# Unread products at the borders of a four-part transformer kernel, with joined loads at its start and another order at the start of its last attention

## The reference

```
x = LN(x + attn0(x))   # 16 heads of 8: softmax(q k^T / sqrt(8) - distance, causal) v, then Wo
x = LN(x + moe(x))     # argmax over 8 experts; LN, 128 -> 512 relu -> 128 of the chosen expert
x = LN(x + attn1(x))   # 16 heads of 64: RMS-normed q, k; bias -distance * omega * softplus(gate(k)); causal
x = LN(x + ffn(x))     # silu gate, two 512x512 gelu layers, 512 -> 128
```

## Time and profile before

| | us |
|---|---|
| median of 3 runs (lowest, highest) | 2205.83 (2204.8, 2212.89) |
| the profiled execution's own time | 2213.37 |
| its span | 2211.6 |
| TensorE busy | 2041.5 (92%) |
| VectorE, ScalarE, GpSimd busy | 1389.9, 1146.0, 839.6 |
| mean granted clock of TensorE | 0.952 |

### The profile page before, as it was taken

One profiled execution on the slowest core, in us unless ns is written; L12 is line 12 of the kernel. 1 busy time (PEld: TensorE's weight loads), 2 busy tenths in 40 slices (PEclk: granted clock), 3 DMA queues, 4 the chain that ended last, 5 costly groups with the idle time before them and its releaser, 6 DMA issues.

```text
span 2211.6 us, 37667 instructions
## 1 busy us (share of the span) xinstructions
PE 2041.5 (92%) x13392; PEld 1231.1 (56%) x13392; DVE 1389.9 (63%) x3316; ACT 1146.0 (52%) x1859; POOL 839.6 (38%) x544
## 2 busy tenths in 40 slices
PE   5799999998487988896999999999999999999998
PEld 3355455554476544454566666666666665656644
DVE  4788888883632787874677777777777764333311
ACT  2366666666344676782455555555555552232232
POOL 5000000001501445442577777777777772000000
PEclk8799999999589999995899999999999999999999
DMA  5233333113165689897477677767776697433300
GB/s 177 104 128 133 134 130 119 59 54 98 65 188 151 187 268 338 270 287 181 105 180 180 154 177 180 182 161 173 178 182 166 168 223 211 110 86 86 91 5 10
DMA packets 260313, 336.09 MB, mean 152 GB/s; under 512 B 22732, under 2 KB 181756, under 8 KB 259720
## 3 DMA queue, kind: packets, MB, share of 16 engines
q1 hardware_dynamic: 244824, 305.82, 51.6%
q0 software_dynamic: 7664, 24.39, 3.1%
q10 hardware_dynamic: 7640, 3.48, 0.6%
HBM read 193.69 MB, written 122.62 MB: 143 GB/s over the span
## 4 chain that ended last, share of the span: by engine, by line
PE 49%; DMA 2%; SPq 2%; DVE 0%; ACT 0%; issue 0%; DVEq 0%
PE ps L959 11%; PE ps L1296 10%; PE ps L910 7%; PE ps L941 6%; PE ps L942 6%; PE ps L1247 2%; PE ps L947 1%; PE ps L1307 1%; PE ps L922 1%; PE ps L1284 1%; PE ps L1285 1%; SPq L1171 1%; DMA a1QA<-a1QB 1%; DMA a1FQ<-s_q 1%; DMA s_y<-a1raw 0%; DMA fyb<-s_y 0%
## 5 line engine op out<-in xcount | busy, mean ns | idle before, releaser
L1132 POOL TENSOR_TENSOR a1sum<-a1sum,a1prob 128x1024 f32<-128x1024 f32 (+3 forms) x256 | 461.3, 1802 | 101.7 <-ACT a1prob L1075 69.7
L1075 ACT ACTIVATE a1prob<-ps 128x512 f32<-128x512 f32 (+2 forms) x640 | 322.7, 555 | 239.1 <-PE ps L947 206.3
L480 DVE TENSOR_REDUCE a0grid<-ps 128x8 f32<-128x1024 f32 x288 | 346.6, 1222 | 99.4 <-PE ps L350 48.8
L581 ACT ACTIVATE a0prob<-ps 128x1024 f32<-128x1024 f32 x288 | 291.3, 1027 | 159.0 <-PE ps L376 89.2
L1011 DVE CUSTOM_DVE_ANT_0 ps<-ps,c_mask_ij 128x128 f32<-128x128 f32 x496 | 264.6, 551 | 92.0 <-issue 87.7
L959 PE MATMUL ps<-a1prob,a1V 128*64 128x512 f32 (+3 forms) x1536 | 275.5, 501 | 4.9 <-ACT a1prob L1075 4.9
L941 PE MATMUL ps<-a1QA,a1KA 69*128 69x512 f32 (+3 forms) x768 | 272.3, 362 | 4.0 <-DMA a1QA<-a1neg 4.0
L942 PE MATMUL ps<-a1QB,a1KB 128*128 128x512 f32 (+3 forms) x768 | 264.9, 353 | 0.0
L910 PE MATMUL ps<-a1KA,a1QA 68*128 68x128 f32 x744 | 229.4, 385 | 5.0 <-DMA a1KA<-s_g 4.3
L959 PEld LDWEIGHTS ps<-a1prob,a1V 128*64 128x64 f32 x1536 | 103.3, 139 | 174.4 <-issue 140.2
L1014 DVE TENSOR_REDUCE a1mx<-ps 128x1 f32<-128x320 f32 x248 | 146.0, 589 | 60.0 <-PE ps L910 57.2
(11 more groups left out here) (269 smaller groups left out, 3191.7 us busy)
## 6 DMA issues: line engine op xcount, KB each, us to landing
a1FQ<-s_q SPq DMA_DIRECT2D x128, 256.0 KB, 7.8
a1KB<-s_k SPq DMA_DIRECT2D x128, 256.0 KB, 8.6
s_xs<-c_zero POOLq DMA_DIRECT2D x19, 1024.0 KB, 8.9
s_q<-mqkT SPq DMA_DIRECT2D x32, 512.0 KB, 4.0
s_v<-mv SPq DMA_DIRECT2D x32, 512.0 KB, 5.8
s_k<-a1KH SPq DMA_DIRECT2D x32, 512.0 KB, 4.9
s_k<-a1KL SPq DMA_DIRECT2D x32, 512.0 KB, 5.9
a1KA<-s_k SPq DMA_DIRECT2D x64, 256.0 KB
```

The costliest lines, as they stand in the source:

```text
L480: dve.tensor_reduce(grid[g % 2][:, :, a:b + 1:b - a], banks(("max", k)), axis=AX.X, op=ALU.max).then_inc(s1_free, 1)
L581: act.activation(prob[:, :, a:b + 1:b - a, :], banks(("exp", q)), ACT.Exp).then_inc(p_full, 1)
L1075: act.activation(weights_of(g, u)[:, group[0]:group[-1] + 1, off:BANK], both(e, u, group), ACT.Exp).then_inc(weighed, 1)
L1132: pool.tensor_tensor(t[:, :, off:BANK], t[:, :, off:BANK], weights_of(g, u)[:, :, off:BANK], ALU.add).then_inc(summed, 1)
```

## The change

1. A new function, `pass_time`, is one fp32 product of the identity with a broadcast of itself into a bank that nobody reads. It stands on TensorE at these places: once per chunk of the routing ahead of `rank`, with the wait on `picked` now ahead of it; eight times after the totals; thirteen times behind the experts, ahead of the wait for their outputs; at n == LAST one of half size after each of the 24 maximum products and one of full size after the turn.
2. The scratch of `attention0` holds three rows of parts per head, so that a head's operand is one block of 24 rows: q as high, high, low and k as high, low, high. A chunk is stored with six DMAs, and a buffer is loaded with two of 48 rows or four of 24.
3. BK of group 0 is loaded on SP's queue behind Q, and `load_second(1)` goes from chunk 5 to behind the row of group 0.
4. At the end of the projections VectorE does six maxima before the gates instead of twelve; TensorE has eight, a gate transpose, one, a gate transpose, and the rest.
5. In group 0 of `attend_and_finish` the maxima begin in unit 4, the turn and the row are one unit later, ACT's two splits stand behind units 4 and 6, VectorE's low part at unit 8, and SP issues the slopes first and v behind q.

```
+def pass_time(nc, const, bank, tiles):
+    ident = const["ident"]
+    nc.tensor.matmul(bank[:, 0:tiles * P], ident[:, :], ident[:, :].unsqueeze(1).to_broadcast([P, tiles, P]), start=True, stop=True)
...
-            for h in range(H):
-                part(engine, buf, name, g, h, done)
+            b, k = divmod(g, per)
+            for m in range(PAIR):
+                row, to, n = 3 * dim * (k * H + m * PAIR), base_of(m) + FIRST, 3 * dim * PAIR
+                engine.dma_start(buf[to:to + n, :].bitcast(F32), scr[name][row:row + n, b * seq:(b + 1) * seq]).then_inc(done, 16)
...
-                for r, part in enumerate((high, low)):
+                for s, part in enumerate(((high, high, low), (high, low, high))[n]):
...
             batch_stored(sp, 0)
+            sp.wait_ge(cleared_first, 1)
             still(sp, Q[0], "q0", 0, loaded1[0])
+            moving(sp, BK[0], "k0", 0, loaded1[0])
...
-                if c == 5:
-                    sp.wait_ge(cleared, 3)
-                    load_second(sp, 1)
...
-                if 0 < g and g + 1 < GROUPS:
-                    sp.wait_ge(s2_full, NU * g)
+                if g + 1 < GROUPS:
+                    if g > 0:
+                        sp.wait_ge(s2_full, NU * g)
+                    else:
+                        sp.wait_ge(cleared, 3)
                     load_second(sp, g + 1)
...
-            act.wait_ge(cleared_first, 1)
-            batch_stored(act, 0)
-            moving(act, BK[0], "k0", 0, loaded1[0])
...
-    share0 = ([0, 0, 2, 3, 3, 4, 4, 4, 4, 0, 0, 0], [0, 0, 0, 0, 0, 0, 0, 0, 0, 3, 3, 3])
+    share0 = ([0, 0, 0, 0, 4, 5, 5, 5, 5, 0, 0, 0], [0, 0, 0, 0, 0, 0, 0, 0, 0, 0, 4, 5])
...
             for h in range(2):
                 copy_high(1, h)
                 load_a(1, h)
-            load_e(1)
             for k in range(PARTS):
                 load_f(2, k)
+            load_v(1)
...
-                    if u == TILES and g + 2 < G:
+                    if u == (TILES if g > 0 else TURN) and g + 2 < G:
                         lower(g + 2, 0)
...
-                    if g + 2 < G and u in (0, 3):
-                        split(g + 2, (0, 3).index(u))
+                    behind = (0, 3) if g > 0 else (4, 6)
+                    if g + 2 < G and u in behind:
+                        split(g + 2, behind.index(u))
...
+                if 0 < i - 3:
+                    pe.wait_ge(picked, i - 3)
                 if 0 <= i - 3:
+                    pass_time(nc, const, ps[:, 5, :], TILES)
                     rank(i - 3)
...
+            for _ in range(8):
+                pass_time(nc, const, ps[:, 6, :], TILES)
...
+            for _ in range(13):
+                pass_time(nc, const, ps[:, 7, :], TILES)
             pe.wait_ge(ye_full, NT)
...
+                    if n == LAST and kind == "max":
+                        pass_time(nc, const, ps[:, 0, :], 2)
+                    if n == LAST and kind == "turn":
+                        pass_time(nc, const, ps[:, 0, :], TILES)
...
-                    first_maxima(range(NM // 2))
+                    first_maxima(range(AHEAD))
```

More of the change, by code:

```diff
@@ L151, in batch_stored @@
             for c in range(b * seq // CHUNK, (b + 1) * seq // CHUNK):
-                engine.wait_ge(stored[c % PARTS3], 16 * 4 * (c // PARTS3 + 1))
+                engine.wait_ge(stored[c % PARTS3], N_STORE * (c // PARTS3 + 1))
         def load_first(engine, g):
@@ L168, in still, with moving @@
         def still(engine, buf, name, g, done):
-            for h in range(H):
-                part(engine, buf, name, g, h, done)
-        def moving(engine, buf, name, g, done):
-            for h in range(H):
[L176 to L185, removed]
+            b, k = divmod(g, per)
+            for m in range(PAIR):
+                row, to, n = 3 * dim * (k * H + m * PAIR), base_of(m) + FIRST, 3 * dim * PAIR
+                engine.dma_start(buf[to:to + n, :].bitcast(F32), scr[name][row:row + n, b * seq:(b + 1) * seq]).then_inc(done, 16)
+        def moving(engine, buf, name, g, done):
+            b, k = divmod(g, per)
+            for h in range(H):
+                row, to, n = 3 * dim * (k * H + h), base_of(h // PAIR) + FIRST + 3 * (h % PAIR) * dim, 3 * dim
+                engine.dma_start(buf[to:to + n, h % PAIR, :].bitcast(F32), scr[name][row:row + n, b * seq:(b + 1) * seq]).then_inc(done, 16)
         def load_x(part):
@@ L195, in store @@
                 nc.sync.wait_ge(low_full, 2 * c + n + 1)
-                for r, part in enumerate((high, low)):
-                    nc.sync.dma_start(scr[name][r, :, c * CHUNK:(c + 1) * CHUNK], part[c % PARTS3][:, n, :].bitcast(F32)).then_inc(stored[c % PARTS3], 16)
+                rows_of = scr[name].rearrange("(h s d) n -> h s d n", s=3, d=dim)
+                for s, part in enumerate(((high, high, low), (high, low, high))[n]):
+                    nc.sync.dma_start(rows_of[:, s, :, c * CHUNK:(c + 1) * CHUNK], part[c % PARTS3][:, n, :].bitcast(F32)).then_inc(stored[c % PARTS3], 16)
         def sync_program():
@@ L576, in exponentials @@
                     for r in range(PARTS3):
-                        act.wait_ge(stored[r], 16 * 4 * len(range(r, chunks, PARTS3)))
+                        act.wait_ge(stored[r], N_STORE * len(range(r, chunks, PARTS3)))
                 if g > 0:
@@ L810, in load_e, with load_v @@
             nc.sync.dma_start(KA[b][EXT:EXT + 4, :, :].bitcast(F32), slopes).then_inc(loaded_e[b], 16)
+        def load_v(x):
+            b, (n, m) = x % NB, divmod(x, PAIRS)
+            if x >= NB:
+                nc.sync.wait_ge(valued, unit(x - NB, NU - 1) + 1)
             nc.sync.dma_start(V[b][:, :, :], scr["v1"][n * S:n * S + S, m * P:m * P + P].rearrange("(t p) n -> p t n", p=P)).then_inc(loaded_v[b], 16)
@@ L848, in sync_program @@
         def sync_program():
+            load_e(1)
             for h in range(2):
@@ L1105, in scalar_program @@
                         keep_den(g - 1)
-                    if u == (TURN if g > 0 else TURN + 2) and g + 1 < G:
+                    if u == (TURN if g > 0 else TURN + 3) and g + 1 < G:
                         row(g + 1)
@@ L1990, in middle @@
         assert turn_gates[LAST]
+        AHEAD = 6
         line = []
@@ L2000, in middle @@
                 here.append((("xT", "gate")[n % 12 // 11], n // 12 + 1, 0))
-            here += [("max", k, 0) for k in range(NM // 2)] if n == LAST else []
-            here += [("aug", c, 0) for c in turn_gates.get(n, ())]
-            here += [("max", k, 0) for k in range(NM // 2, NM)] + [("turn", 0, 0)] if n == LAST else []
+            here += [("max", k, 0) for k in range(AHEAD + 2)] if n == LAST else []
+            for k, c in enumerate(turn_gates.get(n, ())):
+                here += [("aug", c, 0)] + ([("max", AHEAD + 2 + k, 0)] if n == LAST else [])
+            here += [("max", k, 0) for k in range(AHEAD + 2 + len(turn_gates[n]), NM)] + [("turn", 0, 0)] if n == LAST else []
             after_item[n] = here
@@ L2195, in tensor_last @@
                     multiply(n)
-                for _ in after_item[n]:
+                for kind, a, _ in after_item[n]:
                     job(k)
                     k += 1
+                    if n == LAST and kind == "max":
+                        pass_time(nc, const, ps[:, 0, :], 2)
+                    if n == LAST and kind == "turn":
+                        pass_time(nc, const, ps[:, 0, :], TILES)
         def pair(n):
@@ L2364, in vector_last @@
                         gates_b(event_of[EVENTS[n - late][0]])
-            first_maxima(range(NM // 2, NM))
+            first_maxima(range(AHEAD, NM))
             first_row()
```

12 lines of the change are left out of this document (7 added, 5 removed).

## The result

The changed kernel takes 2184.39 us in the median of four runs (2182.59 to 2186.1), the kernel before 2209.36 (four runs, 2204.8 to 2215.85) beside it: a ratio of 0.9885, 95% interval 0.9854 to 0.9915, 25 us less. On another chip, in a later comparison, it was 0.9884 (0.9864 to 0.9903). It is faster, and by a quarter less than the 34 us forecast; the time lies 2 us above the forecast's own range (2162 to 2182) and inside the wide one (2155 to 2196).

The account below looks back on a forecast made before the run. TensorE, busy 92% of the span, was taken as the bound, with stretches at half clock. Terms 10 + 0 + 1 + 3 + 2 + 18 = 34 us gave 2179 against the profiled execution, 2172 as median; range 2155 to 2196.

Parts of the forecast that it names:

- Start: First attention's start: earlier BK loads 4 us, shorter row wait 4, full clock behind it 3, extra stores -1: gain 10.
- Routing: Products ahead of the ranks: hidden in the ranks' wait at full clock; taken 0, bounds 5 us slower to 3 faster.
- Totals: Eight unread products after the totals fit in 11.05 us of standing: gain 1 us, bounds 3 either way.
- border: Behind the experts: thirteen unread products covered by 13.89 us of standing, first projections at full clock: gain 3 us.
- End of the projections: Maximum products before the last attention: unread products covered at full clock, gates' transposes wait less: gain 2 us.
- Group 0: Last attention's first group: two waits gone 9.2 us, clock 15, less 6 for the late `a1FQ` load: gain 18.
- Rival A: Barrier before group 0: passes don't hold the clock; gain 22 us, time 2184; chance 0.20 together with D.
- B: First attention's start gives nothing, extra stored bytes eating the saved issues; gain 24 us, time 2182; chance 0.13.
- C: Half clock where the passes stand, so they cost time: 10 us slower, 2216; chance 0.07.
- D: The split's load eats group 0's gain, leaving 6 to 8 us; time 2183; chance 0.20 together with A.
- A clock once lost stays lost: Dense TensorE stretches, start and group 0: half clock persists despite full activity; rival A therefore costs 12 us, not 4.
- The signs: Trace checks: clock slices, first L350 and L382 times, wq products at 1.9, group 0 at 35 to 39 us, split waiting.

Follow-up runs that it names:

- the two orders alone: Kernel before with only the new orders at the end of the projections and in group 0, no unread products, old start: ratio 0.9956.
- the start alone: Kernel before with only three-part scratch, joined loads, BK on SP's queue and load_second(1) behind the first row: ratios 0.9953 and 0.9947.

## Why the prediction was right or wrong

The time, 2184.39 us, lies in the range and on the forecast side; by the ratio it is 25 us where 34 were forecast. The sum came as near as it did partly by luck: the start gave more than its term in the trace, and group 0 and the routing gave less. Point by point:

- *Start, 10 forecast.* 15 in the trace, 10 to 12 timed alone. The mechanism held, the shares didn't: I gave 4 to the move of `load_second`, which is worth at most about 1 once the loads are joined. Six issues took 2.4 us and not 3.4. Of the price of the larger loads the good end came: TensorE starts 3.8 us behind the last issue of BK, not 9.9.
- *Routing, 0 forecast.* A loss of 1 to 2, within the bounds. The failed step is "a pass at full clock is hidden in the ranks' wait". It stands behind the wait on `picked`, so the wait doesn't cover it; and the clock fell to half there with the passes too.
- *Totals 1, border 3 forecast.* 0.5 and 0.8. The eight were covered as worked out. At the border the clock was down when wq came, 3.76 us as before, behind a stand of 2.65 us that was left after the thirteen. So the step "I expect all to" run at full held for the thirteen (11.3 us), and what it was to buy, the first projections at 1.88, didn't come.
- *End of the projections, 2 forecast.* 1.6 to 2, about as forecast. The clock went up as expected. With the old order it is worth nothing there, with the new one about 1 us; the rest is the handing over with VectorE.
- *Group 0, 18 forecast.* 13 in the traces, against the long form of before. The two waits went, 9.2 us, as said, and a new one of 1.12 us came. The clock term is the one that was mis-sized: 15 less 6, where 4 came. And its cause was wrong: the two orders alone give 40.5 us in group 0, the passes alone 47.0 and nothing in time. What brought the clock up in group 0 was the orders, not the passes before the barrier; that it was by the gaps gone from between its products fits the windows (16.56 us busy of 18 against 12.45 of 20.8) but was not tried by itself. The wait for `a1FQ` that I took 6 us off for was there (2.46, 5.99 and 1.74 us of ACT). TensorE's rows show of it only the 1.0 to 2.8 us for `a1QA<-a1QB`.
- *Rival A* (the passes don't hold the clock) is nearest: 22 us and 2184. Its price came out, its mechanism only in part: with the passes of the change the clock held to the barrier or up to 12 us beyond it and then fell.
- *Rivals B, C and D.* B is out (the start alone gives 10 to 12 us), C too (no loss at the end of the projections, at 0.93). Of D a small part came: the 1.12 us at group 2's first maximum, and group 0 gave 13 and not 6 to 8.
- *"A clock once lost stays lost",* on which I let the Trainium skill's rule fall, was too strong. In the changed kernel and in the orders alone it came back inside group 0 (1.00 from 10 to 16 and from 5 to 16 us behind its start) and was lost again (0.50 by 20 and by 18 us); with the old order it stayed down through the second run in some executions and was back early in it in others. The Trainium skill's rule ("TensorE: Matmul & The Clock Gate", Part 1: The HAM clock gate), that activity releases the throttle, describes the window at 0.88 entered from 0.52; the 18.10 us busy of 18.10 at 0.55 above still speak against it being the whole of it.
- *The signs.* Met: the first L350 before 35 us (30.68) and the first L382 before 84 (74.78), 8 and 9 in the two slices of group 0, a wait of ACT's split. Missed: the second slice at 9 (8), wq's products at 1.9 (3.76), group 0 at 35 to 39 us (41.6). Neither of the two signs of being wrong came.

## What to carry to other kernels

A clock is worth what the bound engine makes of it: products that nobody reads held it at 0.87 to 1.00 through a stretch that VectorE paces and gave nothing that the times show, while taking two waits out of the dense stretch behind gave both the waits and a part of the clock. Before filling idle time, look whether the filler stands in front of a wait or behind it; behind it, it is on the path. And when a queue is late, try joining its small transfers before moving one of them: here fewer issues emptied the queue without the move (BK had changed its queue as well). And where the clock of a stretch falls in one of two ways, profile it more than once before pricing it: here the two forms are 7 us apart.

## What the runs showed that was not expected

- The routing without a pass took 33.8 or 33.9 us from first to last ranks on two chips and 41.4 to 43.4 on others, by waits of VectorE of 3 to 4 us, most of which the profile puts down to no engine of the core. It is larger than most terms of this change.
- Group 0 in the old order has two lengths, 47.0 to 48.3 and 53.9 to 55.0 us, with the clock of its second run at 0.92 to 0.95 or 0.54 to 0.55; in the new order all seven profiles are at 40.1 to 41.9.
- Loads of 24 and 48 rows cost 0.40 us each to issue (1.61/4, 0.81/2), less than the 0.56 of an 8- or 16-row load.
